# Weight phase of a Mamba + FP4 feed-forward kernel: the rounding's subtraction goes from VectorE to GpSimd, and the tap diagonals are made and stored on another schedule

## The reference, cut to what matters

```python
x = L0_attn_x                                     # [8, 1024, 512] f32
xn = _layernorm(x)
out = x + mamba(xn, W_in, conv_w, ...) + ffn(xn, w_gate, w_up, w_down)

def fp4_quant_dequant(x):                         # blocks of 16 along the last dim
    scale = maximum(max(abs(xb)) / 6.0, 1e-12)
    xn = xb / scale
    q = _GRID[searchsorted(_MID, abs(xn))] * sign(xn) * scale   # grid 0 .5 1 1.5 2 3 4 6
def fp4_linear(x, w):                             # both operands quantised
    return einsum('bsk,nk->bsn', fp4_quant_dequant(x), fp4_quant_dequant(w))
ffn: fp4_linear(silu(fp4_linear(x, w_gate)) * fp4_linear(x, w_up), w_down)
# mamba: depthwise convolution with 4 taps (conv_w, 1024 channels), then the state-space scan
```

## Time and profile before

| | us |
|---|---|
| three runs | 5530.35, 5539.40, 5541.11 (median 5539.4) |
| profiled execution, its own time | 5534.0 |
| its span | 5532.1 |
| VectorE busy in the span | 4671.0 (84%) |
| GpSimd busy in the span | 3961.5 (72%) |
| phase_w: start of the span to the first DMA of phase_a | 178.18 |

### The profile page before, as it was taken

The page is one execution under the profiler, slowest core; times in us unless marked ns, Lnnn a source line. Parts: engine busy times, 40 slices in busy tenths (PEclk is TensorE's granted clock), DMA queues, the critical chain, the costliest instruction groups (busy, mean ns, idle before and its releaser), DMA issues.

```text
span 5532.1 us, 79462 instructions
## 1 busy us (share of the span) xinstructions
PE 4907.6 (89%) x22020; PEld 3235.2 (58%) x22020; DVE 4671.0 (84%) x5783; ACT 2865.7 (52%) x4719; POOL 3961.5 (72%) x2042
## 2 busy tenths in 40 slices
PE   1699999999999679889989889889898998998967
PEld 1588888888888345555545545545555554554544
DVE  6667676767676099999999999999999999999997
ACT  1111111111111367767677777677776767777755
POOL 4333333333333099999999999999999999999996
PEclk9999999999999889999999999999999999999979
DMA  2111111111111222333222323332323233332222
GB/s 78 31 42 42 42 42 42 42 42 42 42 42 35 89 83 83 99 98 99 92 93 90 114 85 99 97 96 90 97 89 107 90 93 91 108 95 86 89 83 65
DMA packets 292070, 423.42 MB, mean 77 GB/s; under 512 B 33872, under 2 KB 123984, under 8 KB 287584
## 3 DMA queue, kind: packets, MB, share of 16 engines
q1 hardware_dynamic: 291680, 419.02, 24.4%
HBM read 348.62 MB, written 70.29 MB: 76 GB/s over the span
## 4 chain that ended last, share of the span: by engine, by line
DVE 17%; issue 15%; PE 15%; POOL 9%; ACT 9%; DVEq 1%; DMA 0%; POOLq 0%; ACTq 0%; SPq 0%
DVE hs L1155 11%; DVE acc L1169 6%; POOL v L960 6%; PE mm L1217 4%; ACT decay L1121 4%; PE ht L1280 3%; PE mm L1268 3%; PE mm L1226 2%; POOL hw L970 2%; PE yw L1290 1%; DVEq L820 1%; POOL dt L989 1%; ACT L1130 1%; POOL sz L985 1%; PE mm L1234 1%
## 5 line engine op out<-in xcount | busy, mean ns | idle before, releaser
L960 POOL TENSOR_TENSOR v<-u,b_rep 128x1024 f32<-128x1024 f32 x1024 | 2407.4, 2369 | 146.7 <-DVE hs L1155 142.7
L1121 ACT ACTIVATE decay<-dt,a_neg 128x512 f32<-128x512 f32 x2048 | 1392.4, 687 | 748.2 <-DVE hs L1155 733.5
L1280 PEld LDWEIGHTS ht<-ident,hs 128*128 128x128 f32 x6400 | 782.5, 145 | 1189.8 <-issue 682.3
L1155 DVE TENSOR_TENSOR_SCAN hs<-decay,v 128x512 f32<-128x512 f32 x1024 | 1219.0, 1207 | 180.6 <-POOL v L960 121.0
L1155 DVE TENSOR_TENSOR_SCAN hs<-decay,carry,v 128x512 f32<-128x512 f32 x1024 | 1282.8, 1270 | 51.4 <-ACT decay L1121 38.3
L1280 PE MATMUL ht<-ident,hs 128*128 128x128 f32 x6400 | 1019.9, 284 | 306.8 <-DVE acc L1169 158.0
L1169 DVE SCALAR_TENSOR_TENSOR acc<-ht,c_now,acc 128x512 f32<-128x512 f32 x1600 | 1158.5, 724 | 12.8 <-PE ht L1280 11.7
L490 ACT ACTIVATE sg<-gate 128x512 f32<-128x512 f32 (+1 forms) x192 | 108.1, 563 | 1333.9 <-PE up L536 1333.9
L970 POOL TENSOR_TENSOR hw<-hs,c_rep 128x512 f32<-128x512 f32 x448 | 574.3, 1282 | 10.4 <-DVE hs L1155 10.4
L1217 PE MATMUL mm<-x_in,w_in 128*128 128x512 f32 x1024 | 539.7, 637 | 25.2 <-DMA x_in<-xnt_d 17.4
L1268 PE MATMUL mm<-w_out,yt 128*128 128x512 f32 x1024 | 509.2, 603 | 9.3 <-ACT xb L1028 5.8
(11 more groups left out here) (127 smaller groups left out, 7880.4 us busy)
## 6 DMA issues: line engine op xcount, KB each, us to landing
b_rep<-ssm_d SPq DMA_DIRECT2D x512, 256.0 KB, 3.4
tap_diag<-tap_d SPq DMA_DIRECT2D x128, 256.0 KB, 3.5
w_out<-in_L_attn_W_out SPq DMA_DIRECT2D x32, 1024.0 KB, 7.0
rtb<-res_d SPq DMA_DIRECT2D x128, 256.0 KB, 4.2
c_rep<-ssm_d SPq DMA_DIRECT2D x448, 64.0 KB, 3.3
xt<-in_L_attn_x SPq DMA_DIRECT2D x64, 256.0 KB, 2.8
xnt_d<-xntb SPq DMA_DIRECT2D x64, 256.0 KB, 2.7
rt<-in_L_attn_x SPq DMA_DIRECT2D x64, 256.0 KB, 2.6
```

The costliest lines, as they stand in the source:

```text
L960: nc.gpsimd.tensor_tensor(v[k % 2][:, j:j + 2, :], u[g][:, j:j + 2, :], b_rep[k % 4][:, :].unsqueeze(1).broadcast_to([P, 2, CL]), ALU.mult ...
L1121: nc.scalar.activation(decay[n % 3][:, :], dt[g][:, j, :], ACT.Exp, scale=a_neg[:, GD * g + j, s:s + 1]).then_inc(decay_ready, 1)
L1155: nc.vector.tensor_tensor_scan(h[k % 2][:, j, :], decay[n % 3][:, :], v[k % 2][:, j, :], carry[:, s, GD * g + j:GD * g + j + 1] if c.secon ...
L1280: last = nc.tensor.transpose(ht[add_no[k, t] % 2][:, j, :], h[k % 2][:, j, t * P:(t + 1) * P], ident[:, :])
```

## The change

In `phase_w` the fourth operation of the rounding, `t - m`, is taken from VectorE (L132, and L145 for the last step) and issued by GpSimd in front of the scale back, for all 26 steps. GpSimd then waits for its own subtraction on a new semaphore before it scales back. `rounded` counts three operations a step there. `phase_a` makes its `Quant` without the new argument and keeps the old order.

The diagonals of channel group i are made after ScalarE's copy of group 2i (0, 2, ... 14) and not i; store i is issued behind the raw load of step 6 + 2i (6, 8, ... 20) and not i + 8. A diagonal's buffer is still waited for from i = 2 on. The number of diagonals and stores is as before.

```diff
+        self.unbiased = unbiased
+        self.per = 4 if unbiased is None else 3
...
     # scales_beside_round (round likewise)
-        dve.wait_ge(self.rounded, before.at(4, 3))
-        dve.tensor_tensor(t, t, m, ALU.subtract).then_inc(self.rounded, 1)
+        if self.unbiased is None:
+            dve.wait_ge(self.rounded, before.at(4, 3))
+            dve.tensor_tensor(t, t, m, ALU.subtract).then_inc(self.rounded, 1)
...
     def scale_back(self, pool, out, width, n):
-        pool.wait_ge(self.rounded, n.at(4, 4))
+        if self.unbiased is None:
+            pool.wait_ge(self.rounded, n.at(4, 4))
+        else:
+            pool.wait_ge(self.rounded, n.at(3, 3))
+            pool.tensor_tensor(t, t, m, ALU.subtract).then_inc(self.unbiased, 1)
+            pool.wait_ge(self.unbiased, n.at(1, 1))
         pool.tensor_tensor(out..., t..., scale..., ALU.mult).then_inc(self.quantised, 1)
...
-            if s >= 8 and s - 8 < ND:
-                i = s - 8
+            if s >= 6 and s % 2 == 0 and s // 2 - 3 < ND:
+                i = s // 2 - 3
                 sp.wait_ge(diag_set, KC * (i + 1))
                 sp.dma_start(tap_d[i], diag[i % 2][:, :, :]).then_inc(diag_stored[i % 2], 16)
...
-            if g < ND:
-                if g == 0:
+            if g % 2 == 0 and g // 2 < ND:
+                i = g // 2
+                if i == 0:
                     act.wait_ge(taps_loaded, 16)
-                if g >= 2:
-                    act.wait_ge(diag_stored[g % 2], 16 * (g // 2))
+                if i >= 2:
+                    act.wait_ge(diag_stored[i % 2], 16 * (i // 2))
```

More of the change, by code:

```diff
@@ L68, with __init__ @@
 class Quant:
-    def __init__(self, sems, small, t, m):
+    def __init__(self, sems, small, t, m, unbiased=None):
         self.scaled, self.normed, self.rounded, self.quantised = sems
         self.small, self.t, self.m = small, t, m
+        self.unbiased = unbiased
+        self.per = 4 if unbiased is None else 3
     def buffers(self, n, width):
@@ L122, in scales_beside_round @@
         dve.tensor_scalar(scale, top, 1.0 / 6.0, 1e-12, ALU.mult, ALU.max).then_inc(self.scaled, 1)
-        dve.wait_ge(self.rounded, before.at(4, 1))
+        dve.wait_ge(self.rounded, before.at(self.per, 1))
         dve.tensor_scalar(m, m, 1.0, MAGIC, ALU.max, ALU.mult).then_inc(self.rounded, 1)
@@ L126, in scales_beside_round @@
         dve.reciprocal(recip, scale).then_inc(self.scaled, 1)
-        dve.wait_ge(self.rounded, before.at(4, 2))
+        dve.wait_ge(self.rounded, before.at(self.per, 2))
         dve.tensor_tensor(t, t, m, ALU.add).then_inc(self.rounded, 1)
@@ L139, in round @@
                           ALU.bitwise_and).then_inc(self.rounded, 1)
-        dve.wait_ge(self.rounded, n.at(4, 1))
+        dve.wait_ge(self.rounded, n.at(self.per, 1))
         dve.tensor_scalar(m, m, 1.0, MAGIC, ALU.max, ALU.mult).then_inc(self.rounded, 1)
-        dve.wait_ge(self.rounded, n.at(4, 2))
+        dve.wait_ge(self.rounded, n.at(self.per, 2))
         dve.tensor_tensor(t, t, m, ALU.add).then_inc(self.rounded, 1)
-        dve.wait_ge(self.rounded, n.at(4, 3))
-        dve.tensor_tensor(t, t, m, ALU.subtract).then_inc(self.rounded, 1)
+        if self.unbiased is None:
+            dve.wait_ge(self.rounded, n.at(4, 3))
+            dve.tensor_tensor(t, t, m, ALU.subtract).then_inc(self.rounded, 1)
     def scale_back(self, pool, out, width, n):
-        _, scale, _, t, _ = self.buffers(n, width)
-        pool.wait_ge(self.rounded, n.at(4, 4))
+        _, scale, _, t, m = self.buffers(n, width)
+        if self.unbiased is None:
+            pool.wait_ge(self.rounded, n.at(4, 4))
[3 more added lines that the diff above has]
+            pool.wait_ge(self.unbiased, n.at(1, 1))
         pool.tensor_tensor(out.rearrange("p (b k) -> p b k", k=QB), t.rearrange("p (b k) -> p b k", k=QB),
@@ L179, in phase_w @@
     taps_loaded, diag_set, diag_stored = sem("taps_loaded"), sem("diag_set"), [sem(f"diag_stored{p}") for p in range(2)]
-    quant = Quant(q_sems, small, t, m)
+    quant = Quant(q_sems, small, t, m, sem("w_unbiased"))
     steps = [(w_gate[r * P:(r + 1) * P, :], H, gu, r * P) for r in range(NI)]
@@ L253, in _ @@
             nc.scalar.activation(hi, src, ACT.Copy).then_inc(w_hi, 1)
-            if g < ND:
-                if g == 0:
+            if g % 2 == 0 and g // 2 < ND:
+                i = g // 2
+                if i == 0:
                     act.wait_ge(taps_loaded, 16)
-                if g >= 2:
-                    act.wait_ge(diag_stored[g % 2], 16 * (g // 2))
+                if i >= 2:
+                    act.wait_ge(diag_stored[i % 2], 16 * (i // 2))
                 for k in range(KC):
-                    nc.scalar.activation(diag[g % 2][:, k, :], ident[:, :], ACT.Copy,
-                                         scale=taps[:, g, k:k + 1]).then_inc(diag_set, 1)
+                    nc.scalar.activation(diag[i % 2][:, k, :], ident[:, :], ACT.Copy,
+                                         scale=taps[:, i, k:k + 1]).then_inc(diag_set, 1)
     @block.tensor
```

## The result

| | us |
|---|---|
| before, median of 13 runs | 5534.3 (5528.4 to 5541.1) |
| changed, median of 13 runs | 5521.7 (5517.5 to 5525.8) |
| ratio | 0.9978, 95% interval 0.9969 to 0.9986 |
| changed, profiled execution: own time, span | 5520.45, 5518.6 |

The changed kernel is 12.6 us faster. The ratio is that of the changed kernel's time to the one before. The forecast was 6.1 us and a time of 5530; the time lies in the stated range. The gain is about 0.2%, just above the 11 us that I had called the bound of what can be told, and twice what I had summed. The interval (8 to 17 us) does not reach down to 6.1.

A forecast was written before the change was run, and what follows sets the result against it. The first phase was taken as bound by VectorE and GpSimd in turn, with a store stall in six steps. Narrow steps gain 15.0 us, the phase's end loses 8.9: 6.1 gained, forecast 5530 us, range 5513 to 5541.

The forecast's parts named there:

- The diagonals: First phase, six long narrow steps: the stall on stores goes, 9.86 us becomes 4.21 each, 59.14 - 25.2 = 33.9 us.
- The price of the subtraction: GpSimd's new operation: 1.28 us at 512 wide, 3.2 at 1408, plus 0.17 waiting for its own result.
- The order of the two engines: Narrow step: three possible orders of VectorE and GpSimd, at 5.29, 5.15 or 4.81 us; the second was taken.
- the middle order: Narrow step: VectorE's exponent slips in once, between GpSimd's subtraction and scale back; about 5.15 us a step.
- A narrow step: First phase, L130 to L130: 5.15 us each; twenty take 103.0 instead of 118.04, 15.0 less.
- The end of the phase: After the narrow steps: two mixed steps lose 1.9 us, two wide 3.8, the last round 1.6 and 1.6; sum 8.9.
- The stated test: Narrow steps: the prediction is wrong if the stall has gone and the pace is not between 5.0 and 5.3 us.
- rival 1: Narrow step: VectorE keeps the port through L124, 4.81 us a step; gain 14.8, about 5519 to 5524 us; chance 0.24.
- Two thirds of what the diagonals give back is spent: First phase: that share of the diagonals' 33.9 us was said to go on GpSimd's longer turn.
- Rival 3: Narrow step: L128 doesn't stand for GpSimd, the subtraction is hidden, near 4.2 us a step; 5504 to 5509 us; chance 0.10.
- Rival 2: Narrow step: GpSimd is never interrupted, 5.29 us a step; gain 2.2, 5532 to 5537 us; chance 0.16.
- The sign: Whole kernel: faster by 11 us or more 0.40, slower 0.07, within 0.53.

The follow-up runs named there:

- e1: The changed kernel with the subtraction kept on VectorE, leaving the diagonals' new schedule alone; 5500.6 us, ratio 0.9939.
- e4: e1 with diagonals made after every group 0 to 7 as before and store i behind load i + 6; 5500.2 us, ratio 0.9936.
- e3: e1 with VectorE's nudged reciprocal issued ahead of the add of the magic number; 5508.9 us, ratio 0.9955.
- e5: e1 with the rounding's tile w_m in PSUM instead of SBUF, in one buffer; 5495.0 us, ratio 0.9921.
- e7: The changed kernel with the exponents in a PSUM tile of their own and the blocks' maxima in PSUM; 5509.3 us, ratio 0.9952.

## Why the prediction was right, and where it was off

- **The diagonals**: right, in mechanism and size. 33.9 us worked out, 34.2 measured alone (e1). Not foreseen was that moving the stores alone would do (e4).
- **The price of the subtraction**: right. 1.28 and 3.2 from the rows with two whole inputs, 1.26 and 3.15 measured. Its wait for itself was taken at 0.17 and is 0.08 (93.11 to 93.19).
- **The order of the two engines**: right; the middle order (L118 in the gap, L124 held off) holds in the narrow steps, and in the wide step shown too.
- **A narrow step, 5.15 against 4.88**: the term mis-sized. Up to L118's end all is within 0.02 (subtraction's end 2.60 forecast, 2.59 measured; L118's end 2.89 and 2.87). Then "the scale back at 3.94" is 3.79: GpSimd's operation ends 0.92 after the one of VectorE that held it off, and not its whole 1.05. The earlier trace rows had that number: L106 ends (94.06) 0.91 after L132 (93.15). In all these rows an operation that stood ends its own duration less 0.13 to 0.15 after the one that it stood for (0.28 for 0.42, 0.54 for 0.69, 0.92 for 1.05); that its start is done while it stands would explain it, but is not shown. And "from L122 to L130 it is 1.26": a small operation that stood is done when the scale back is, and the next starts 0.05 before; from the scale back's end to the nudge it is 1.09. The two errors make 0.15 + 0.17 = 0.32; 0.05 of it had been taken off beforehand (3.94 + 1.26 is 5.20, put down as 5.15), which leaves the 0.27. Over twenty steps that is 5.5 us of the miss of 6.5.
- **The end of the phase**: 8.9 forecast, 7.9 measured: 1.5 for 1.9 in the two mixed steps, 3.35 for 3.8 in the two wide ones, 3.1 for 3.2 in the last round. In the wide step, 12.3 against 12.09, it is the same two terms: the scale back ends at 9.21 and not 9.35, and from there to the nudge it is 2.88 and not 3.0.
- **The stated test**, "the narrow pace is not between 5.0 and 5.3", came out against me: the mechanism held, the pace did not. My rival 1 (4.81, VectorE goes on through L124) gives nearly the right time for the wrong reason; L124 standing 1.03 us tells the two apart.
- **The time in the range** is in part luck of a wide range: 5513 to 5541 holds the kernel before (5534.3) too, and the outcome "faster by 11 us or more", which came, had 0.40 against 0.53 for "within". Of the 8.3 us between 5530 and 5521.7, 6.5 are the gain mis-summed and 1.8 the base, which I had put at 5536.
- **"Two thirds of what the diagonals give back is spent"** does not follow from its own sum: 18.9 + 8.9 of 33.9 is 82%. Measured it is two thirds (21.6 of 34.2), because the loss was forecast too large.
- **Rival 3** (the add does not stand for GpSimd) is out by the pace, 4.88 and not 4.2; e3 takes its premise, for the subtraction, the same kind of operation on the same tiles. The add itself is seen behind a running GpSimd operation in no row here. Rival 2, the uninterrupted order, fell with L118's place.
- **The sign**: the two parts go opposite ways. The subtraction's move is a loss in every short step; the whole is faster because the other part is larger. e1 beats the changed kernel by 21 us.

What I said of the Trainium skill, page "SBUF — State Buffer", section "Who interferes with whom", holds: no row shown of before had a VectorE operation with two SBUF inputs behind a running GpSimd operation, and e3 shows one (1.43 against 0.69).

## What to carry to other kernels

When work moves from VectorE to GpSimd, don't count who is busy; write down one step with both engines in turn, and mark which VectorE operations stand for a running GpSimd operation. If the chain of those is what ends the step, a longer turn of GpSimd is paid for: here with 0.67 us a narrow step for an operation of 1.26, of which 0.35 came back because VectorE's subtraction no longer holds the normalisation off. An operand in PSUM can be worth more than the faster form of the instruction (e5), and a store behind a load in one queue should stand where the load's wait is already over.

## What the runs showed of the hardware that was not expected

An instruction on 32 columns, 0.17 us alone, stands for the whole of a GpSimd operation as a large one does (L124, 1.03 us). Put the data it reads in PSUM and it takes 0.18 in the middle of a running GpSimd operation (e7):

```profile
60.12 1.06 POOL L165 TENSOR_TENSOR w_q<-w_t,w_small 128x512 f32<-128x512 f32 x1
...
60.60 0.18 DVE L128 TENSOR_SCALAR w_small<-w_top 128x32 f32<-128x32 f32 x1
```

VectorE's scans of the last phase (L1155) run beside GpSimd's operations and seem not to take part. One of their two whole inputs, `decay`, is in PSUM in `phase_b` and the other, `v`, in SBUF, so they are placed as e5's L137. GpSimd's L970 takes 1282 ns on average beside them, and the subtraction of the same size, which no scan overlaps, 1264 in the groups of after:

```profile
L158 POOL TENSOR_TENSOR w_t<-w_t,w_m 128x512 f32<-128x512 f32 x22 | 27.8, 1264 | 0.0
```

No run moved `decay` to SBUF, so that the place of that input is the reason is not shown for the scans.
